# A copy on GpSimd in place of one of the transfers that build the feed forward's input

## The reference

```python
def shift_tokens(t):
    a, s = jnp.split(t, 2, -1)
    s = jnp.pad(s, ((0, 0), (1, 0), (0, 0)))[:, :-1]
    return jnp.concatenate([a, s], -1)
...
for i in range(DEPTH):                       # 6 layers
    x = attn_layer(shift_tokens(x), ...) + x  # 16 heads of 64, window 32, rotary positions
    x = ffn_layer(shift_tokens(x), ...) + x   # layer norm, 128 -> 2 x 341, a * gelu(gate), -> 128
```

## Time and profile before

| what | time or share |
|---|---|
| median of 3 runs | 4441.26 us (4439.8 to 4445.46) |
| the profiled execution | 4439.44 us, span of the core 4438.1 us |
| granted TensorE clock, mean | 0.915 |
| PE busy | 3859.1 us, 87% |
| DVE busy | 3062.1 us, 69% |
| POOL busy | 2649.1 us, 60% |
| ACT busy | 2568.4 us, 58% |
| first stack | from about 827 to 2548 us of the span |
| second stack | from about 2737 to 4433 us |

### The profile page before, as it was taken

The page is one execution under the profiler, slowest core; times in us unless marked ns, Lnnn a source line. Parts: engine busy times, 40 slices in busy tenths (PEclk is TensorE's granted clock), DMA queues, the critical chain, the costliest instruction groups (busy, mean ns, idle before and its releaser), DMA issues. The chain is left out here.

```text
span 4438.1 us, 158857 instructions
## 1 busy us (share of the span) xinstructions
PE 3859.1 (87%) x66864; PEld 2706.7 (61%) x66864; DVE 3062.1 (69%) x6301; ACT 2568.4 (58%) x4921; POOL 2649.1 (60%) x2218
## 2 busy tenths in 40 slices
PE   7968694399999999999999623999999999999996
PEld 5645453266667666676676422676666676766764
DVE  4446464678777777777777347777777777777773
ACT  3325251266666676666676401666667676666664
POOL 2029074477667676676776203776766767767662
PEclk7569797699999999999999855999999999999998
DMA  0010100133332333333322101333323333233222
GB/s 15 1 33 1 35 1 5 45 93 78 83 85 70 90 80 82 81 82 78 83 65 71 45 7 35 93 82 81 91 65 90 80 85 85 73 87 83 64 71 55
DMA packets 307779, 280.48 MB, mean 63 GB/s; under 512 B 158840, under 2 KB 205696, under 8 KB 307072
## 3 DMA queue, kind: packets, MB, share of 16 engines
q1 hardware_dynamic: 307072, 270.33, 23.9%
HBM read 55.22 MB, written 1.05 MB: 13 GB/s over the span
## 5 line engine op out<-in xcount | busy, mean ns | idle before, releaser
L1459 ACT ACTIVATE m_sq<-PS 128x512 f32<-128x512 f32 x384 | 226.2, 595 | 197.6 <-PE PS L1312 160.8
L1459 ACT ACTIVATE l_sq<-PS 128x512 f32<-128x512 f32 x384 | 226.2, 595 | 196.5 <-PE PS L1312 160.1
L1724 POOL TENSOR_TENSOR l_Pm<-l_Pm,l_rs 128x1024 f32<-128x1024 f32 x96 | 182.9, 1905 | 238.2 <-DVE l_rs L1596 238.2
L1724 POOL TENSOR_TENSOR m_Pm<-m_Pm,m_rs 128x1024 f32<-128x1024 f32 x96 | 182.9, 1905 | 233.7 <-DVE m_rs L1596 233.7
L124 POOL TENSOR_TENSOR rstd<-rstd,minus_half 128x4 f32<-128x4 f32 x40 | 41.9, 1046 | 378.5 <-DVE rstd L120 378.5
L1614 DVE TENSOR_TENSOR XN<-PS,XN 128x128 f32<-128x128 f32 x192 | 56.2, 293 | 279.4 <-PE PS L1364 279.3
L1583 DVE TENSOR_TENSOR l_QR<-PS,l_rot 128x512 f32<-128x512 f32 x192 | 131.8, 687 | 163.2 <-ACT l_sq L1459 163.2
L1583 DVE TENSOR_TENSOR m_QR<-PS,m_rot 128x512 f32<-128x512 f32 x192 | 131.8, 686 | 163.0 <-ACT m_sq L1459 163.0
L1719 POOL TENSOR_TENSOR m_QR<-m_QR,m_UQ 128x1024 f32<-128x1024 f32 x96 | 227.7, 2372 | 24.0 <-DVE m_UQ L1586 24.0
L1719 POOL TENSOR_TENSOR l_QR<-l_QR,l_UQ 128x1024 f32<-128x1024 f32 x96 | 227.7, 2372 | 23.3 <-DVE l_UQ L1586 23.3
L1719 POOL TENSOR_TENSOR l_KR<-l_KR,l_UK 128x1024 f32<-128x1024 f32 x96 | 227.0, 2364 | 0.2 <-DVE l_UK L1586 0.2
(11 more groups left out here) (388 smaller groups left out, 11840.8 us busy)
## 6 DMA issues: line engine op xcount, KB each, us to landing
l_V<-l_Vt SPq DMA_DIRECT2D x576, 128.0 KB
m_V<-m_Vt SPq DMA_DIRECT2D x576, 128.0 KB
l_V<-l_Vt SPq DMA_DIRECT2D x384, 64.0 KB
m_V<-m_Vt SPq DMA_DIRECT2D x384, 64.0 KB
l_wqkv<-l_wqkv_dram SPq DMA_DIRECT2D x72, 128.0 KB, 2.4
m_wqkv<-l_wqkv_dram SPq DMA_DIRECT2D x72, 128.0 KB, 2.5
l_rot<-l_rot_dram SPq DMA_DIRECT2D x24, 256.0 KB, 3.8
m_rot<-l_rot_dram SPq DMA_DIRECT2D x24, 256.0 KB, 3.8
```

Of the source, the lines that this page charges most:

```text
L1459: ac.activation(sq[:, c, b * 512:(b + 1) * 512], PS[:, 2 * c + b, :], ACT.Square).then_inc(sq_out)
L1724: gp.tensor_tensor(pm, pm, over(rs[:, :], 2, [P, 16, 2 * LW]), ALU.mult).then_inc(pn_out)
```

## The change

POOL gets a new step `keep_same(g)`, which copies the 64 features that stay from `Y` to `xsh`. The transfer of L1807 goes. The sum that DVE waits for in `shifted` falls by 16 a group, and DVE waits for the new semaphore `same_out` as well. POOL does the copy in step 4g+5, ahead of the rotary sum of q, while SP keeps the shifted features in step 4g+4.

```diff
                     def statistics(g):
-                        ve.wait_ge(shifted, 64 * (g // 2 + 1) + 48 * ((g + 1) // 2))
+                        ve.wait_ge(shifted, 48 * (g // 2 + 1) + 32 * ((g + 1) // 2))
+                        ve.wait_ge(same_out, g + 1)
                         V.wait()
...
+                    def keep_same(g):
+                        gp.wait_ge(y_add, 4 * g + 4)
+                        at_ge(gp, xnorm_out, g - 1)
+                        gp.tensor_copy(xsh[:, g % 2, :, 0:D // 2], group(Y, g % NG)[:, :, 0:D // 2]).then_inc(same_out)
+
...
                             keep_halo(s + 1)
+                        measured = phase(s, 5)
+                        if measured is not None:
+                            keep_same(measured)
                         if s + 2 < NL:
                             add(s + 2, 0)
...
-                        measured = phase(s, 5)
                         if measured is not None:
                             root(measured)
...
                         at_ge(sp, xnorm_out, g)
-                        sp.dma_start(xsh[:, par, :, 0:D // 2], Y[:, tiles, 0:D // 2]).then_inc(shifted, 16)
                         sp.dma_start(xsh[1:P, par, :, D // 2:], Y[0:P - 1, tiles, D // 2:]).then_inc(shifted, 16)
```

More of the change, by code:

```diff
@@ L1187, in build @@
         nT_out, gelu_out, XST_out = signals("l_nT_out l_gelu_out l_XST_out")
-        fvar_out, fmid_out, xnorm_out, h_out, f_add, froot_out = signals("l_fvar_out l_fmid_out l_xnorm_out l_h_out l_f_add l_froot_out")
+        same_out, fvar_out, fmid_out, xnorm_out, h_out, f_add, froot_out = signals("l_same_out l_fvar_out l_fmid_out l_xnorm_out l_h_out l_f_add l_froot_out")
         v_spread, w_attn, w_rot, w_ffn, shifted = signals("l_v_spread l_w_attn l_w_rot l_w_ffn l_shifted")
```

## The result

| | before | after |
|---|---|---|
| median of 16 runs | 4441.28 us | 4424.10 us |
| lowest to highest | 4432.8 to 4448.5 | 4417.0 to 4441.6 |
| profiled execution, span | 4438.1 us | 4424.1 us |

The ratio is 0.9963, with a 95% interval of 0.9952 to 0.9973: 16 us faster, between 12 and 21. I had forecast 7 us with a range that ended at 4426, so the direction was right and the size was not.

A forecast was written before the change was run, and what follows sets the result against it. PE, busy 87% of the span, was taken as the bound, gaining only where it waits for V behind SP's queue. 11.1 us gained less 3.9 lost gave 7.2 net, 4434.1 us forecast, range 4426 to 4446.

The forecast's parts named there:

- SP's queue, not the data: At the shift, the removed transfer costs its issue time on SP, which makes V's transfers late, 1.17 us in group 2.
- 0.70 us a group: On SP, one issue of 0.66 us plus 0.04 goes, so the queue behind it moves 0.70 us forward, 48 times.
- The slow transfer stays and holds SP for 6.50 us: In the shift, L1808 stays at about 18 GB/s over one engine, and L1810's issue stays 6.50 us long.
- The copy costs 0.39 us and is covered but in ten groups, 3.9 us: On POOL, 48 copies of 0.39 us; only ten groups behind the rotary tables lack idle time, 3.9 us lost.
- in more than 10 groups: Sign that the prediction is wrong: PE waits for POOL's Pm in more than 10 groups.
- What the 0.70 us are worth: 11.1 us: Gain from SP's earlier queue: 5.4 us in the first stack, 4.3 in the second, 1.4 at the two ends.
- The wall: After V, PE's turn of `O` waits for ACT's gapless chain, capping each group's gain at its room; 29 groups gain zero.
- V is not delayed: Rival: the shift does not delay V's transfers; only the ends gain 1.4 us, POOL's 3.9 stay, 4443.8 us; chance 0.15.
- The turn of O is no wall: Rival: ACT's chain moves too, 17.7 us gained less 3.9, 4427.5 us; chance 0.18 shared with SP gaining 1.15 us (4430.8).
- Slower, in the chain: Rival: POOL's copy enters the chain from statistics to `O`, 48 times 0.39, 18.7 us, giving 4458.6 us; chance 0.08.
- The copy is much dearer: Rival: POOL's copy takes 1 us each, so the ten groups cost 10 us, giving 4440.2 us; chance 0.07.
- same: Outcome class for the whole kernel: time within about 0.2%, 8.9 us, of before, counted as no change; chance 0.58.

The follow-up runs named there:

- tiny_last: The changed kernel plus a 4 KB transfer on SP issued behind the shifted transfers; ratio to the kernel before 0.9974, and 0.9984 when repeated.
- before_split: The kernel before with its slow shifted transfer cut in two, 112 partitions and 15; ratio 0.9926, 33 us faster.
- before_order: The kernel before with L1807 issued behind the shifted transfers, no POOL copy; ratio 0.9993, 3 us faster.
- drop_only: The kernel before without the transfer of the 64 features that stay and without any copy, so they stay zero; ratio 0.9947, 24 us faster.
- before_tiny: The kernel before plus a 4 KB transfer on SP ahead of L1807; ratio 1.0058, 26 us slower.
- after_tiny: The changed kernel with a 4 KB transfer on SP where the removed 128 KB one was; ratio to the kernel before 0.9999.
- pool_only: The kernel before with all its transfers, plus POOL's copy into a spare tile; ratio 1.0005, 2 us slower.

## Why the prediction was wrong in size

*SP's queue, not the data.* Right. A transfer of 4 KB in the same place takes the whole gain away, twice 0.9999. That V alone carries the gain, which the sum assumed but for the ends, is not: tiny_last keeps about half of it with V as late as before.

*0.70 us a group.* Right for V: SP's lateness for it fell from 1.19 to 0.48 us. L1808 itself moved by more, 0.88 us (3.80 to 2.92), against 0.70 at the ends (from 0.73 to 0.03 us after `Y`). The difference fits SP's stalls falling less often ahead of the shift: in the changed kernel L1808 starts with the least delay outside the ends, 2.3 us, in 12 groups, in the kernel before with the corresponding 3.0 in two.

*The slow transfer stays and holds SP for 6.50 us.* Right, and shown by before_split.

*The copy costs 0.39 us and is covered but in ten groups, 3.9 us.* Right within what can be measured: POOL waits at least 1.8 us before Pm in the 36 other groups. After, in group 1 of the second stack, POOL works without a gap through the copy:

```profile
2905.65 0.40 POOL L1712 COPY m_kT<-m_kT 128x256 f32<-128x256 f32 x1
2905.99 0.41 POOL L1730 COPY m_xsh<-XN 128x256 f32<-128x256 f32 x1
2906.35 2.39 POOL L1720 TENSOR_TENSOR m_QR<-m_QR,m_UQ 128x1024 f32<-128x1024 f32 x1
2908.67 1.93 POOL L1725 TENSOR_TENSOR m_Pm<-m_Pm,m_rs 128x1024 f32<-128x1024 f32 x1
```

PE's wait for Pm rose by 4.3 us in the whole (3.9 forecast), in 12 waits instead of 10. The two more, 1.5 us, stand at the starts of the stacks, where there is no copy, and one of 1.37 us is there in the second profile of the kernel before too; so the sign "in more than 10 groups" is not given. In the ten groups the wait went from 11.3 to 14.1 us, 2.8 more, and before_order, which has no copy, has 12.7 there: the size of this term is not fixed better than that. Beside the copy DVE was at work that reads PSUM in the groups with idle time, as I had said; in the ten it was in sums over one tile (L1593 and L1601), which took their usual 1.20 and 1.16 us.

*What the 0.70 us are worth: 11.1 us.* This is the step that failed. The removal is worth 24 us (17 to 30) by drop_only, about 20 by the change plus POOL's cost (16 and 4). I gave each group the smallest of 0.70, the room ahead of the turn of `O` and SP's lateness, and so 29 of 46 groups nothing. Removed or added, 0.70 us a group moved the end by three quarters of the whole. What the traces show of the difference:

1. It is not that I had one execution only. Groups do change: in group 20 of the first stack PE waits 0.8 us for `O` in the first profile of the kernel before and 1.1 us for V in the second. But the same sum worked out from the second profile, without the three small parts, gives 5.1 + 5.6 = 10.7 us for the two stacks, against 5.5 + 4.0 = 9.5 from the first. The rule was too small, not the sample.
2. The wall was used somewhat too strictly. In the first pair of profiles the wait for V fell by 12.7 us (about 16 forecast) and that for `O` rose by 0.4, so 12.3 net; in the second pair V fell by 12.8 and `O` rose by 1.5, so 11.3. The sum had 9.7. This is 2 to 3 us of the miss. That there is a wall at all is seen in before_split, and in before_tiny, where V is nearly always last and the wait for `O` falls to 6.8.
3. I priced a wait at its length. After the longest ones the granted clock falls, to 0.63 over four microseconds in group 16, and the matmuls behind run longer. The earlier trace rows has the sign of it, L1334 with 2.05 us where 1.48 is the rule, and I passed over it. PE's busy time fell by 2.3 us in the first pair and by 4.1 in the second (3868.8 to 3864.7), L1318 alone by 3.7 and 7.2 over both stacks. The second profile of before has 9.7 us more busy time than the first, so this term has the right sign twice but no sure size.
4. What an earlier start of the slow transfer is worth, apart from V, was put at 1.4 us at the ends and up to 0.44 us in three groups. tiny_last kept 7 to 12 us of the gain by it, and no wait in its profiles shows the way. This part of the cause stays open.

For the first pair of profiles the terms make 12.3 us (V less `O`) + 1.5 (the ends) + 2.3 (PE's busy time) + 2.0 (PE's pauses within L1334, 30.3 to 28.3) - 4.3 (Pm) = 13.8, of 14.0 measured. For the second they make 11.3 + 1.5 + 4.1 + 10.7 (38.9 to 28.2) - 4.8 (10.9 to 15.7) = 22.8, of 22.0. PE's pauses within L1334 scatter from 27.6 to 38.9 us over all profiles without a clear tie to the change. So these sums show where the time lies in each execution; they don't show that the change caused each term.

*The rivals.* "V is not delayed" (4443.8) is excluded by drop_only and after_tiny, and SP's lateness for V fell by 0.70 us; its idea that the slow transfer matters by itself is not excluded, see tiny_last. "The turn of O is no wall" (4427.5) came nearest in number and had 0.18 with its neighbour; it is not right as a mechanism, since the wait for `O` grows in before_split. "Slower, in the chain" (4458.6) is excluded by pool_only. "The copy is much dearer" fell with the 0.405 us.

*The border.* The change is clear of the 0.2% that I called the limit, so "same", which had 0.58, was wrong too, and the range should have gone lower: its bound took every wait for V at 0.70 or its length, 17.7 us, and left out what items 3 and 4 name.

## What to carry to other kernels

Where many nearly equal paths race in a periodic schedule, a value built from the room of each period can be far too small: here it was 11.1 us where 24 (17 to 30) were measured, and a second trace gave the same. Take such a sum as a low value and the shift times all periods (34 us here) as the most, and let the range reach over both. A queue that issues transfers is a resource like an engine: count what each issue puts late behind it, whatever its size. And look first at the slowest item in that queue: here a partition count of 127, cut into 112 and 15, was worth twice the change that was made.

## What was not expected of the hardware

- The issue of a 768-byte transfer held SP for 6.50 us behind a transfer over 127 partitions at 18 GB/s, and 0.76 us once that was cut in two.
- A wait of 3.46 us on PE was followed by a granted clock of 0.63 (mean of four microseconds) and a projection that took 3.30 us in place of 1.98; after a wait of 1.14 us it stayed at 1.00.
- The lateness of one queue reached the end by about three quarters in either direction: 24 us (17 to 30) for 0.70 us a group taken away, 26 us (19 to 32) for 0.70 added.
